# Slabs of the edge matrix loaded as eight halves a group instead of four wholes, in the same four places of SBUF

## The reference, cut to what matters

```
m = x @ weight[l]
agg = segment_sum(m[src] * edge_weight, dst)
gi = agg @ w_ih.T + b_ih ; gh = x @ w_hh.T + b_hh
r = sigmoid(i_r + h_r) ; z = sigmoid(i_z + h_z) ; n = tanh(i_n + r * h_n)
x = (1 - z) * n + z * x
```

## Time and profile before

| What | Value |
|---|---|
| Median of three runs | 3301.0 us |
| Span of the profiled execution | 3300.9 us |
| The same execution's own time | not given apart from its span; the three runs are 3299.79 to 3303.86 us |
| TensorE (PE) busy | 2999.7 us, 91% |
| Mean granted TensorE clock | 0.941 |
| DMA, mean over the span | 241 GB/s |
| Layers two and three of the GRU network | about 1089 to 2449 us |

### The profile page before, as it was taken

How to read it: one execution, slowest core, us unless ns; L and a number is a source line. 1 busy time by engine, 2 the same in 40 slices (tenths; PEclk the granted TensorE clock), 3 DMA queues, 4 the chain that set the end, 5 groups by cost and what they waited for, 6 DMA issues and landing times.

```text
span 3300.9 us, 75545 instructions
## 1 busy us (share of the span) xinstructions
PE 2999.7 (91%) x29405; PEld 1914.6 (58%) x29405; DVE 1519.5 (46%) x4507; ACT 904.4 (27%) x2115; POOL 980.1 (30%) x1214
## 2 busy tenths in 40 slices
PE   6999999999999987878789787878889999999998
PEld 5888888888888533434345333434345555555554
DVE  7888888888887233434342343434442001001111
ACT  5666666666665100000001001001022001001111
POOL 3222223222323344655551464554520000000000
PEclk8999999999999988878889888888889999999999
DMA  5655555555532866657577565746656876877885
GB/s 192 266 230 242 231 237 238 236 236 233 242 127 76 343 237 231 252 200 275 184 280 283 220 231 212 267 177 258 223 221 240 306 302 254 304 301 269 299 307 186
DMA packets 150125, 796.32 MB, mean 241 GB/s; under 512 B 19300, under 2 KB 29480, under 8 KB 136200
## 3 DMA queue, kind: packets, MB, share of 16 engines
q1 hardware_dynamic: 119960, 729.87, 56.3%
q0 software_dynamic: 27344, 54.53, 5.7%
q10 hardware_dynamic: 2720, 10.62, 0.8%
HBM read 567.97 MB, written 226.97 MB: 241 GB/s over the span
## 4 chain that ended last, share of the span: by engine, by line
PE 90%; issue 8%; DVE 1%; ACT 1%; DMA 0%; POOL 0%; another core or an unknown queue 0%; ACTq 0%; DVEq 0%; POOLq 0%
PE ps L923 28%; PE ps L1127 24%; PE ps L1206 18%; PE ps L1199 11%; PE ps L933 2%; PE ps L934 2%; PE ps L1219 1%; PE ps L935 1%; PE ps L936 1%; PE ps L1220 1%; PE ps L1106 1%; ACT ring L1602 0%; PE ps L1073 0%; PE ps L1221 0%; PE ps L1222 0%
## 5 line engine op out<-in xcount | busy, mean ns | idle before, releaser
L923 PE MATMUL ps<-ring,Y 128*128 128x448 f32 x2352 | 927.8, 550 | 145.6 <-issue 145.5
L836 POOL DMA_INDIRECT ring<-y_rows,ring x700 | 673.5, 962 | 683.4 <-DVE ring L1738 410.7
L923 PEld LDWEIGHTS ps<-ring,Y 128*128 128x128 f32 x2352 | 453.6, 193 | 594.8 <-issue 594.8
L1127 PE MATMUL ps<-ring,Y 128*128 128x448 f16 x4116 | 780.6, 352 | 0.0
L1602 ACT ACTIVATE ring<-ps 128x392 f16<-128x392 f32 (+1 forms) x1568 | 654.1, 504 | 303.6 <-PE ps L1199 297.1
L1127 PEld LDWEIGHTS ps<-ring,Y 128*128 128x128 f16 x4116 | 402.7, 98 | 373.8
L1206 PE MATMUL ps<-ring,Y 128*128 (+1 forms) x2744 | 613.9, 366 | 3.4 <-issue 2.9
L1738 DVE SCALAR_TENSOR_TENSOR ring<-ring 128x128 f32<-128x128 f32 x1384 | 402.1, 347 | 350.3 <-DMA ring<-y_rows,ring 223.8
L1206 PEld LDWEIGHTS ps<-ring,Y 128*128 128x128 f32 x2744 | 490.5, 189 | 19.3 <-issue 4.1
L1199 PEld LDWEIGHTS ps<-shared 64*128 64x128 bf16 x18816 | 341.3, 94 | 132.7 <-ACT ring L1602 87.0
L1199 PE MATMUL ps<-shared 64*128 64x49 bf16 (+1 forms) x18816 | 391.1, 191 | 22.4 <-issue 10.3
(11 more groups left out here) (188 smaller groups left out, 1309.6 us busy)
## 6 DMA issues: line engine op xcount, KB each, us to landing
ring<-adj_w SPq DMA_DIRECT2D x72, 2688.0 KB
adj_w<-ring SPq DMA_DIRECT2D x48, 2744.0 KB, 12.2
ring<-adj_h SPq DMA_DIRECT2D x42, 2800.0 KB, 9.4
ring<-adj_h SPq DMA_DIRECT2D x42, 2688.0 KB, 9.1
adj_h<-ring SPq DMA_DIRECT2D x56, 1372.0 KB, 5.0
ring<-adj_w SPq DMA_DIRECT2D x24, 2912.0 KB
ring<-y_rows,ring POOLq DMA_INDIRECT x700
y_rows<-Y ACTq DMA_DIRECT2D x2, 2560.0 KB, 10.9
```

The source lines that it names most:

```text
L836: pool.indirect_dma_start(out=run_rows[:, i % ROW_BUFS, :], out_offset=None, in_=y_rows, in_offset=bass.IndirectOffsetOnAxis(ap=run_edges[ ...
L923: mm = pe.matmul(ps[:, bank, 0:GW], Y[:, h, :], slab(s)[:, :, h - h0, :], start=(h == 0), stop=(last and h == TILES - 1))
L1127: mm = pe.matmul(ps[:, par, 0:GW], part[:, h, :], counts_slab(par, s)[:, :, h - h0, :], start=(h == 0 and part is Y_high), stop=(h == TILE ...
```

## The change

The slabs become eight of 7, 6, 6, 6, 6, 6, 6 and 6 tiles. Each place holds two of them, one behind the other (`SLAB_AT`), so the places, their order and the tiles in them stay. Each half has its own DMA, its own semaphore and its own count in `s_used`, which goes to eight a group. Where the program named slabs by number (splits of an aggregate, the first loads, the hand-over to the counts), it names the halves of the same places.

```diff
-SLAB_TILES = [(0, 13), (13, 25), (25, 37), (37, 49)]
+SLAB_TILES = [(0, 7), (7, 13), (13, 19), (19, 25), (25, 31), (31, 37), (37, 43), (43, 49)]
 SLABS = len(SLAB_TILES)
 SH = 13
+PLACES = 4
+PER_PLACE = SLABS // PLACES
+SLAB_AT = [7 * (s % PER_PLACE) if s < PER_PLACE else 6 * (s % PER_PLACE) for s in range(SLABS)]
...
         def slab(s):
-            return ring[:, (s + SLABS // 2) % SLABS]
+            h0, h1 = SLAB_TILES[s]
+            return ring[:, (s // PER_PLACE + PLACES // 2) % PLACES, :, SLAB_AT[s]:SLAB_AT[s] + h1 - h0, :]
...
             def dense_slab(layer, g, s):
                 h0, h1 = SLAB_TILES[s]
                 sp.wait_ge(s_used, SLABS * (layer * DENSE + g) + s + 1)
-                sp.dma_start(slab(s)[:, :, 0:h1 - h0, :].rearrange("p u h c -> p u (h c)"),
+                sp.dma_start(slab(s).rearrange("p u h c -> p u (h c)"),
                              strips(adj_w)[:, bass.ds(PARTS * g, PARTS), h0 * SUB:h1 * SUB])\
                   .then_inc(s_slab[s], 16)
...
-                        sp.wait_ge(s_used, SLABS * (N_LAYERS - 1) * DENSE + HALVES * r + s + 1)
+                        sp.wait_ge(s_used, SLABS * (N_LAYERS - 1) * DENSE + PER_PLACE * (HALVES * r + s + 1))
...
-                aggregate(0, 0, slabs=range(1), chunks_of=1)
+                aggregate(0, 0, slabs=range(PER_PLACE), chunks_of=1)
...
-                aggregate(DENSE - 1, 1, slabs=range(SLABS - 1))
+                aggregate(DENSE - 1, 1, slabs=range(SLABS - PER_PLACE))
                 gates(DENSE - 2, 0, DENSE - 2)
-                aggregate(DENSE - 1, 1, slabs=range(SLABS - 1, SLABS))
+                aggregate(DENSE - 1, 1, slabs=range(SLABS - PER_PLACE, SLABS))
```

More of the change, by code:

```diff
@@ L384, in gnn_program @@
             .rearrange("p (b h c) -> p b h c", h=TILES, c=SUB)
[L385 to L386 removed]
+        ring = ring_flat[:, 0:PLACES * PARTS * SH * SUB].rearrange("p (s u h c) -> p s u h c", s=PLACES, u=PARTS, h=SH)
+        counts_at = [PLACES // 2 * PARTS * SH * SUB, 0]
         counts_size = HALVES * PARTS * HH * SUB // 2
         def slab(s):
[L390 removed]
+            h0, h1 = SLAB_TILES[s]
+            return ring[:, (s // PER_PLACE + PLACES // 2) % PLACES, :, SLAB_AT[s]:SLAB_AT[s] + h1 - h0, :]
         def counts_slab(r, s):
@@ L412, in gnn_program @@
         run_sizes = [ROW_BUFS * P, RUNS * WIN * P, ROUNDS * 3, WIN * ROUNDS]
-        run_at = [SLABS * PARTS * SH * SUB + sum(run_sizes[:i]) for i in range(5)]
+        run_at = [PLACES * PARTS * SH * SUB + sum(run_sizes[:i]) for i in range(5)]
         assert run_at[-1] <= (WIN * STRIPS_PER_GATHER + 1) * ROW
@@ L1002, in second_gru_layer @@
                 node_chunks(1, 3, 7, SECOND_BANKS)
-                aggregate(0, 0, slabs=range(1), chunks_of=1)
+                aggregate(0, 0, slabs=range(PER_PLACE), chunks_of=1)
                 node_chunks(1, 7, NC, SECOND_BANKS)
-                aggregate(0, 0, slabs=range(1, SLABS), chunks_of=1)
+                aggregate(0, 0, slabs=range(PER_PLACE, SLABS), chunks_of=1)
                 pe.wait_ge(s_mat, 16)
@@ L1020, in second_gru_layer @@
                 node_chunks(2, 2, 4, THIRD_BANKS)
-                aggregate(GROUPS, 0, slabs=range(1), chunks_of=2, skipped=SKIPPED)
+                aggregate(GROUPS, 0, slabs=range(PER_PLACE), chunks_of=2, skipped=SKIPPED)
             def last_gru_layer():
@@ L1028, in last_gru_layer @@
                 node_chunks(2, 4, first, THIRD_BANKS)
-                aggregate(n0, 0, slabs=range(1, 2), chunks_of=2, skipped=SKIPPED)
+                aggregate(n0, 0, slabs=range(PER_PLACE, 2 * PER_PLACE), chunks_of=2, skipped=SKIPPED)
                 node_chunks(2, first, NC, THIRD_BANKS)
-                aggregate(n0, 0, slabs=range(2, SLABS), chunks_of=2, skipped=SKIPPED)
+                aggregate(n0, 0, slabs=range(2 * PER_PLACE, SLABS), chunks_of=2, skipped=SKIPPED)
                 pe.wait_ge(s_mat, 32)
                 for i in range(DENSE // 2):
-                    early = range(3 if i == DENSE // 2 - 1 else SLABS)
+                    early = range(SLABS - PER_PLACE if i == DENSE // 2 - 1 else SLABS)
                     aggregate(n0 + 2 * i + 1, 1, slabs=early, skipped=SKIPPED)
```

## The result

The changed kernel takes 3320.38 us (median of 4 runs, 3319.26 to 3325.86), the kernel before 3300.39 us in the same set (4 runs, 3296.66 to 3303.86). The ratio is 1.0066, 95% interval 1.005 to 1.0082: slower by 20 us. The forecast was 3375 us, slower by 74. The sign was right and the time lies in the range, but the cost is about a quarter of what was forecast.

What follows compares the result with a forecast made beforehand. TensorE bounds the kernel, with a hole in each steady group that ends behind POOL's gathers. 18 groups x 3.8 = 68 us plus 3 us for each first burst, 74 us on 3301.0, give 3375 us; eight-in-ten range 3262 to 3445.

Steps and rivals of the forecast that it cites:

- the stall: End of each of 18 steady GRU groups, called the hole: PE does only 8 matmuls in 16 us, the rest "issue" idle.
- the release: Stall's end, when SP sees the hung counts: 46.6 us behind the gathers' start, 5.1 behind POOL's stop; forecast not to move.
- the bracket: In a burst of POOL's gathers, counts begin to hang between 13.3 and 17.8 us after its start.
- the full-rate stretches: Runs of aggregate matmuls on PE at 0.377 us each before the hole: 18 alike, some 36.5 us each.
- The step that failed: Steady groups: count at 17.5 us hangs, PE slows 4.5 us earlier, ten of 12 instructions stay behind: 3.8 us a group.
- the two first bursts: First gather bursts of layers two and three, which hang on their second count already: 3 us each.
- More transfers: SP issues eight slab DMAs a group instead of four; SP has time and no half is late: 0 us.
- The size of the pieces: Slab pieces fall from 5824 and 5376 bytes to 3136 and 2688: 0 in steady groups.
- More waits on TensorE: Four more waits a group on slabs that lie ready, before matmuls: 0 to 3 us in all, taken as 0.
- A: Rival, no change: onset belongs to POOL's burst or PE's position, whatever the counts; 3301 us, chance 0.23.
- B: Rival, faster: shorter slab transfers let gathers land sooner, the hanging path fills later; 3240 us, 3010 without hole, chance 0.22.
- C: Rival, much slower: the number of pieces fills the path, onset 9 us forward, 24 instructions undone; 3490 us, chance 0.12.

Runs made afterwards that it cites:

- before_ten_gathers: Kernel before without the row gathers of layers two and three except eleven (last two groups' sums wrong): 2951.3 us, ratio 0.8951.
- drain10_third: Kernel before, but POOL waits every ten rounds until its last gather has landed, in the last set: 3200.63 us, ratio 0.9638.
- counts_only: Changed kernel with four whole slab transfers and four waits, keeping only the eight counts of use: 3299.28 us, ratio 1.0 against the kernel before.
- transfers_only: Changed kernel with eight transfers and waits but four counts, both halves of a place issued together: 3311.5 us, ratio 1.0036 against the kernel before.
- eight_by_parts: Kernel before with eight transfers a group, cut by 128-row parts so pieces stay whole; counts and issue times as before: 3308.57 us, ratio 1.0037.
- sixteen_third: Kernel before with sixteen transfers a group, four for each place, issued in fours at the times of before, last set: 3342.6 us, ratio 1.0076.
- waits_at_places: Changed kernel with TensorE waiting for both halves of a place ahead of its first matmul: 3324.74 us, ratio 1.0076 against the kernel before.
- late2_third: Kernel before with the next group's slabs 0 and 1 issued only once slab 2 is used, last set: 3385.05 us, ratio 1.0192.
- two_transfers: Kernel before with two transfers a group (25 and 24 tiles), each issued when both its slabs are used, set without the stall: 2952.32 us, 1.004.

## Why the prediction was right and wrong

**What bounds the kernel.** Right: the stall, 16 us in each of 18 groups, is TensorE's idle time, it comes from POOL's gathers, and it ends about 5 us behind their stop. before_ten_gathers and drain10_third show the first two by taking them away, and the release of the kernel after the third. Right too was the bracket, 13.3 to 17.8 us: where the stall is, a count due some 17 us into a burst hung. Two readings of the rows were off: the full-rate stretches of the kernel before are not "each some 36.5 us long" but 33.8 to 36.5, and by the prediction's own figures SP's issue at 1264.11 is 0.4 us behind the end of slab 0 (1263.7), not 0.2.

**The step that failed** is the one that I let decide: "PE then falls out of its rate 8.1 us behind it, 4.5 us earlier ... with 12 more instructions of the aggregate undone." I had taken the distance between a hung count and the fall of the rate from one stall and made it a cause. The distance is not fixed: over the 18 groups of the kernel before it is 6.0 to 8.7 us behind the third slab's count, and after the change 9 to 13 us behind the fifth count, with no fall at all in one group. The counts did hang as forecast, but 2.9 instructions more were left undone, not 12, and counts_only, which has the counts and not the transfers, lost nothing. One price stands: at 0.377 us an instruction, 2.9 are 1.1 us against the measured 0.99 a group; at the forecast's ten they were 3.8. The step was wrong, not what a lost instruction costs. The 3 us that I put on each of the two first bursts came out as +0.1 and -1.9.

**More transfers.** I put them at nothing in the steady groups. By transfers_only and eight_by_parts they, with the waits that go with them, are half of the cost, 10 or 11 us, and sixteen_third shows the cost grow with their number. My reason, that SP has time and the slabs are not late, looked only at what a transfer delays by itself, not at what it does to the stall. Without the stall the reason holds: sixteen transfers cost nothing (0.9999). The size of the pieces is nothing, as forecast.

**More waits on TensorE.** I took nothing. For their place that holds, by waits_at_places; for their number it holds without the stall, where sixteen cost nothing, and stays open beside it.

**The rest, 9 to 13 us,** comes only with transfers and counts together (1.0066 and 1.0076 against 1.0036), that is when SP issues the halves at times of their own, the first at 5.6 us into the group in place of 10.2. Neither alone has it. Why is open: early traffic was my theory, and late2_third, the run that was to test it, moved the traffic the wrong way and does not settle the matter.

**The rivals.** A said that the onset belongs to POOL's burst whatever counts there are; of counts alone that is what counts_only shows, but the kernels with more transfers move it. B did not occur: they make the stall earlier, not later; no stall at all, which it put at 3010 us, is 2940 us, of which some 18 us lie in the first layer. C (the pieces fill the path) had the right direction at a wrong place: more transfers, not more pieces, and a tenth of the price.

**Open.** What holds the counts up, whether it is a path that fills at all, and why it happens in some sets of runs and not in others, no run here shows. The first layer's 18 us say that these sets differ in something beside the gathers. In the trace only the late counts, the slow matmuls and VectorE's steps show it; none of them names it. I also did not have two_transfers in a set with the stall, so whether fewer transfers than four help there is not known.

## What to carry to other kernels

When idle time is "issue" while another engine gathers rows, first find out what ends it and take that away in a run of its own; a distance read from one stall is a coincidence until a second group shows it. Do not split transfers that are on time: it gained nothing in either kind of set here, and beside gathers that stall the kernel each further transfer a group added 2 to 2.7 us to the whole time. A pause in a long burst of gathers can pay (0.9638) or cost (1.0813), so measure it where the kernel is to run.

## What the runs showed of the hardware

- The same kernel took 2940 us in two sets and 3300 to 3319 us in four, within 0.3% of itself in each; some 340 of the 360 us lie in the two layers with the stall. The profile of one set says little about the other.
- In a burst of gathers at 1.25 us each, TensorE and VectorE can stop nearly altogether (8 matmuls in 16 us) while POOL keeps its pace; without the stall the same pace holds for 48 us beside a full TensorE.
- A pause after every ten gathers until they had landed (2.3 to 4.8 us in the group shown) took the stall away in all 18 groups.
- A semaphore count can be seen 26 us late (49.6 against 23.6 us into the group) while the engine that raised it goes on: in that group PE kept its full rate until 1522.2 (1489.47 + 32.70), 9 us behind the moment at which the count was due.
- Two pieces that lie next to each other in memory went out as one packet here: splitting them in the description left 119960 packets.
